# Attention on one core: the main steps in pairs, with sums of two steps one behind the other

## The reference, cut to what matters

```python
qkv = x @ Wqkv + bqkv
q, k, v = jnp.split(qkv, 3, axis=-1)
q, k, v = (heads(q), heads(k), heads(v))
scores = jnp.einsum('bhid,bhjd->bhij', q, k) * scale
scores = scores + alibi_causal_bias(s, NUM_HEADS)
attn = jax.nn.softmax(scores, axis=-1)
out = jnp.einsum('bhij,bhjd->bhid', attn, v)
out = out.transpose(0, 2, 1, 3).reshape(b, s, NUM_HEADS * HEAD_SIZE)
return out @ Wo + bo
```

## Time and profile before

| | |
|---|---|
| median of three runs | 1863.14 us |
| profiled execution, its own time | 1878.28 us |
| profiled execution, span | 1876.6 us |
| mean granted TensorE clock | 0.941 of full |
| TensorE busy | 1682.8 us (90%) |
| TensorE weight loads busy | 1100.5 us (59%) |
| VectorE busy | 941.6 us (50%) |
| ScalarE busy | 590.7 us (31%) |
| GpSimd busy | 647.8 us (35%) |

### The profile page before, as it was taken

How to read it: one execution, slowest core, us unless ns; L and a number is a source line. 1 busy time by engine, 2 the same in 40 slices (tenths; PEclk the granted TensorE clock), 3 DMA queues, 4 the chain that set the end, 5 groups by cost and what they waited for, 6 DMA issues and landing times. The chain is left out here.

```text
span 1876.6 us, 22879 instructions
## 1 busy us (share of the span) xinstructions
PE 1682.8 (90%) x8402; PEld 1100.5 (59%) x8402; DVE 941.6 (50%) x1575; ACT 590.7 (31%) x809; POOL 647.8 (35%) x527
## 2 busy tenths in 40 slices
PE   6996899999999999999697999939999995499997
PEld 5884444444444444444275777727777773388886
DVE  7653756466666566654143555625654454122322
ACT  3210144444444344445221212234324321122221
POOL 4000223677785886600034666624110101000000
PEclk9997699899999899999798999979999997799999
DMA  7756524344535343500373112134230210802210
GB/s 239 239 196 179 91 68 108 95 99 107 140 79 113 115 103 88 132 4 10 108 239 101 59 61 68 47 103 140 69 113 1 90 46 23 297 6 85 90 45 22
DMA packets 97589, 188.41 MB, mean 100 GB/s; under 512 B 26810, under 2 KB 36682, under 8 KB 95610
## 3 DMA queue, kind: packets, MB, share of 16 engines
q1 hardware_dynamic: 72350, 119.59, 22.7%
q0 software_dynamic: 13648, 51.61, 9.1%
q10 hardware_dynamic: 11488, 15.82, 2.6%
HBM read 121.84 MB, written 64.90 MB: 100 GB/s over the span
## 5 line engine op out<-in xcount | busy, mean ns | idle before, releaser
L925 DVE TENSOR_REDUCE att_maxes<-att_unit 128x1 f32<-128x512 f32 (+3 forms) x640 | 385.9, 611 | 269.5 <-PE att_unit L795 152.7
L907 ACT ACTIVATE att_probs<-att_scores 128x1024 f32<-128x1024 f32 (+1 forms) x320 | 285.6, 895 | 386.6 <-PE att_scores L824 189.4
L841 PE MATMUL att_outp<-att_probs,att_vs 128*64 128x512 f32 (+3 forms) x1280 | 310.2, 564 | 0.0
L795 PE MATMUL att_unit<-moew_wbh,moew_wah 100*128 100x512 f32 (+2 forms) x320 | 149.0, 482 | 9.9 <-DMA moew_wbh<-alibi_k_rounded 5.3
L1465 PE MATMUL glu_u<-glu_xh,glu_w 128*128 128x512 f32 x352 | 138.3, 393 | 18.7 <-DMA glu_xl<-zn_lo 18.7
L795 PE MATMUL att_unit<-moew_wbl,moew_wal 100*128 100x512 f32 (+2 forms) x320 | 142.9, 454 | 0.5
L1466 PE MATMUL glu_u<-glu_xl,glu_w 128*128 128x512 f32 x352 | 137.9, 392 | 0.0
L795 PEld LDWEIGHTS att_unit<-moew_wbh,moew_wah 100*128 100x128 f32 x320 | 65.4, 207 | 119.2 <-DVE att_maxes L925 81.2
L795 PEld LDWEIGHTS att_unit<-moew_wbl,moew_wal 100*128 100x128 f32 x320 | 62.4, 197 | 121.8 <-DVE att_maxes L925 79.5
L1524 DVE TENSOR_TENSOR glu_hid<-glu_sig,glu_u 128x512 f32<-128x512 f32 x44 | 30.3, 688 | 168.1 <-ACT glu_sig L1504 168.1
L824 PE MATMUL att_scores<-moew_wal,moew_wbl 102*128 102x512 f32 (+2 forms) x320 | 108.3, 411 | 3.3 <-ACT att_probs L907 3.3
(11 more groups left out here) (276 smaller groups left out, 3439.7 us busy)
## 6 DMA issues: line engine op xcount, KB each, us to landing
att_q_raw<-in_w POOLq DMA_DIRECT2D x48, 352.0 KB, 3.8
w_ternary<-att_q_out POOLq DMA_DIRECT2D x24, 352.0 KB, 2.6
glu_w<-w_ternary ACTq DMA_DIRECT2D x9, 768.0 KB, 10.6
xn<-qkv_x SPq DMA_DIRECT2D x4, 1024.0 KB, 6.7
q_hi<-qkv_hi SPq DMA_DIRECT2D x16, 256.0 KB, 4.0
q_lo<-qkv_lo SPq DMA_DIRECT2D x16, 256.0 KB, 4.4
k_hi<-qkv_hi SPq DMA_DIRECT2D x16, 256.0 KB, 2.6
k_lo<-qkv_lo SPq DMA_DIRECT2D x16, 256.0 KB, 3.3
```

The costliest lines, as they stand in the source:

```text
L795: last = pe.matmul(unit[:, h, 0:cover], qs[par][0:SROWS, h, t * P:(t + 1) * P], ks[par][0:SROWS, h, g * CH:g * CH + cover], start=True, st ...
L841: last = pe.matmul(outp[v_cols(h), c % 2, off:CH], vs[p % 2][:, kt, v_cols(h)], probs[:, g % 4, h, off:CH], start=kt == 0, stop=kt == TT * ...
L907: act.activation(probs[:, g % 4, :, off:CH], scores[:, g % 2, :, off:CH], ACT.Exp).then_inc(exped, 1)
L925: dve.tensor_reduce(maxes[:, h, t, g:g + 1], unit[:, h, 0:width], AX.X, ALU.max).then_inc(unit_taken, 1)
```

## The change

The loop over main steps goes in twos. For steps `g` and `g + 1`, with unit positions `early = g + 22` and `late = g + 23`, the order is now: scores of `g`; both halves of `early`; scores of `g + 1`; the first half of `late`; the sums of `g - 2` and of `g - 1`; the second half of `late`. At a turn, which always falls on `late`, the turn stands behind the scores of `g + 1`, and both halves of `late` behind the sums. Behind the last unit steps only scores of two steps and sums of two steps are left. Number and form of all instructions stay the same, and so do the programs of the other engines.

```diff
-            for g in range(NG):
-                v = g + LEAD
-                now = turns_before(v)[1]
+            for g in range(0, NG, 2):
+                early, late = g + LEAD, g + LEAD + 1
+                early_turns, late_turns = (turns_before(v)[1] for v in (early, late))
                 score(g)
-                for n in now:
-                    turn(n, v)
-                if v < NG and not now:
-                    unit_product(v, 0)
-                if g > 1:
+                for n in early_turns:
+                    turn(n, early)
+                if early_turns:
+                    score(g + 1)
+                    turned_before(early)
+                if early < NG:
+                    unit_product(early, 0)
+                    unit_product(early, 1)
+                if not early_turns:
+                    score(g + 1)
+                for n in late_turns:
+                    turn(n, late)
+                if early < NG and not early_turns and not late_turns:
+                    unit_product(late, 0)
+                if g:
                     sums(g - 2)
-                if v < NG:
-                    if now:
-                        turned_before(v)
-                        unit_product(v, 0)
-                    unit_product(v, 1)
+                    sums(g - 1)
+                if early < NG:
+                    if early_turns or late_turns:
+                        turned_before(late)
+                        unit_product(late, 0)
+                    unit_product(late, 1)
             sums(NG - 2)
             sums(NG - 1)
```

## The result

The changed kernel takes 1883.65 us (median of 11 runs, 1877.27 to 1898.31) against 1866.18 us of the kernel before (11 runs, 1859.78 to 1874.88). The ratio is 1.0092, 95% interval 1.0065 to 1.0119: 0.9% slower. The forecast was 1889, in the range 1866 to 1908.

The account below looks back on a forecast made before the run. TensorE was taken to bound the loop; halved switches gain 38 us, but 65 us of waits and stalls outweigh them, in all about +26: 1904 us profiled, 1889 as a median. Range 1866 to 1908.

Parts of the forecast that it names:

- What bounds the kernel: Attention loop: TensorE sets the pace, busy 84.5 of 84.7 us in an undisturbed pair of heads.
- the loads put down to VectorE: Unit products' weight loads, 160.7 us in 229 cases in the table of waits; claimed not to be waits in common steps.
- the price of the switch: TensorE changing between score or unit products and sums, and back: 0.26 us, which the change saves per pair of steps.
- the wait of e1: Second unit product of the earlier position waits for VectorE's reduction of the previous pair's last unit: 0.35 us a pair.
- The term of 38 us: Gain over all 160 pairs of steps from halving the switches between kinds of product, 0.24 us each with masks.
- The turn: Transposition of the maxima, moved ahead of all sums: an unstalled one gets a wait of about 0.63 us.
- Stalls: Turn's short VectorE operations held up by GpSimd: the new order has no reserve against them and loses 6 us more.
- The clock: TensorE's clock may fall more often behind longer waits at turns: up to +15 us, in the range only.
- Sum: Whole kernel: +3.1 us per pair of heads makes +23.1, less 2.6 at the end, plus 6 for stalls: +26.
- rival (b): Waits and gain balance within 0.5%: waits cost two thirds of the count, +5 us, 1868 us; chance 0.12.
- Rival (a): VectorE keeps up, at the earlier position's second unit product and at turns; only the gain remains, -38: 1825 us; chance 0.09.
- Rival (c): The price sits at each step's sums, not at the switch, so nothing is saved: 1928 us; chance 0.03.

Follow-up runs that it names:

- e4_quarter_old: The kernel before, with each row-maximum reduction reading a quarter of its columns and the exponential scaled by 0.01: 1862.58 us, ratio 0.9909 to the kernel before.
- e3: The changed kernel, with each row-maximum reduction reading a quarter of its columns and the exponential scaled by 0.01: 1836.09 us, ratio 0.9772 to the kernel before.
- e6: The changed kernel without GpSimd's arithmetic for the ternary weights, which are copied as they are: 1861.55 us, ratio 0.9959 to the kernel before.
- e7: The kernel before without GpSimd's arithmetic for the ternary weights, which are copied as they are: 1859.02 us, ratio 0.9948 to the kernel before.
- e9: The changed kernel with the turn's cast and subtraction replaced by three one-input reductions: 1864.91 us, ratio 0.9969 to the kernel before.
- e11: The kernel before with the turn's cast and subtraction replaced by three one-input reductions: 1855.58 us, ratio 0.9922 to the kernel before.
- e1_turn_mid: The changed kernel with the turn between the two steps' sums instead of ahead of both: 1870.63 us, ratio 0.9953 to the kernel before.

## Why the prediction was right, and where it was off

- *What bounds the kernel.* Right. That the loads put down to VectorE were the price of the switch was argued from rows 3 to 5; e4_quarter_old shows it. One of the arguments was weak, that a wait for VectorE would vary: the wait of e1, a real one, repeats as exactly (after the change steps 14 and 15 take 4.35 or 4.36 us in seven of the eight pairs of heads; the eighth ran them at 1.2 GHz).
- *The price of the switch* was mis-sized: 0.36 us for a pair of steps and not 0.26. I took the 0.48 of the first sum as the price of any and counted only the last one's 0.05 more; the inner ones take 0.43. The term of 38 us is up to 57 by e3 and e4 (an estimate, 160 x 0.36; some pairs with masks give 0.29).
- *e1's wait of 0.35.* Right to 0.01. With the gain at 0.36 a whole pair breaks even instead of losing 0.09, and the pairs of steps outside the turns gain 0.9 us in a pair of heads where I had a loss of 1.1 (3.1 less the turns' 2.0).
- *The turn.* 0.63 forecast, 0.62 measured. The four pairs with a turn are 2.0 longer; my 2.0 were the turns' waits alone, with a wait of e1 and a gain of the pairing to come, and those two nearly cancel.
- *Stalls.* The mechanism was right. The differences of e6 and e7, and of e9 and e11 (less the chain's 6), put the stalls with all that came of them at 14 to 15 of the 17.5 us. The stalls proper were about as priced: of the loop's 21.2 us some 10 are the clock's and 6 the order's own, which leaves 5 where I had 6. The idle time at the turns gives a higher figure, 20 us more than before, of which 10 stay once the unstalled turns of e6 and e7 (13.3 and 2.8) are taken off.
- *The clock* was the term left out of the sum. I had it in the range alone, with up to 15 us; it took about 10 in the profiled executions, one of each kernel.
- *Sum.* +26 us forecast, 20.5 for the order and 6 for stalls; +17.5 measured. The order itself cost 3 to 6 us, so it was priced some 15 too high, because the gain of the switch was priced up to 19 too low; the clock made up for most of that. That the total came so near is in part luck, and without the clock's share the kernel would by this estimate be only some 0.4% slower, which is my rival (b). Rival (a) named the right place to look at, the wait of e1; it was not hidden. The ordinary pairs do balance by themselves, as (b) had it. Rival (c) is refuted by e3 against e4.

## What to carry to other kernels

Before moving an engine's work closer together, write down for each buffer half how long a release takes (start of the reader, its duration, the wake-up) and what of other work lies between its two writes; a grouping that saves switches also removes that cover, and here it took back all of a gain of up to 57 us. Long waits at stalled turns also had falls of the clock beside them, which cost as much as the waits: count such waits even where they are rare. Where a table names an engine for a wait, look whether that engine was still at work when the wait ended: at the first unit behind the sums VectorE had long been done, at e1 it had not, though both repeat to the hundredth in every pair. And an operation that has a fixed place, as the turn here, goes to where the most other work lies between its last input and itself: between the two blocks of sums an unstalled turn waited for nothing, though it splits the block in two. In e1_turn_mid the last sum ahead of such a turn takes 0.53 us to its successor instead of 0.43, and the first behind it 0.05 more than inside a block.

## What the runs showed of the hardware that was not expected

A block of sums costs about 0.36 us for switching in and out, whether it holds four matmuls or eight (e3 against e4). The cast and the two-input subtraction of VectorE, 0.17 us each, took up to 2.53 and 1.57 us beside GpSimd's operations on 128 x 704 elements; in the same place reductions with one input never took over 0.19. The Trainium skill (SBUF — State Buffer, Who interferes with whom) gives a rule by which this is so: a VectorE instruction with at most one input in SBUF and outside the two-port modes does not contend with GpSimd, while a cast can enter a two-port mode, in which the engine that issues first holds the shared ports for its whole instruction, and an instruction with two such inputs contends with one of GpSimd that reads SBUF. The trace agrees on both sides, 2.31 us for the cast that ends with a GpSimd operation of 2.04, and 0.16 to 0.17 for the reductions.
